# One program without barriers between its four stages, with the first query heads moved forward, two rotation buffers and a later turn of the routings

## The reference

```python
x = x + tanh(g_xattn[0]) * L0_xattn(_layernorm(x), ctx, ctx, ...)   # linear attention, 8 heads of 64
x = x + tanh(g_ffn[0])   * L0_ffn(_layernorm(x), ...)               # base product plus low-rank experts
x = x + tanh(g_xattn[1]) * L1_xattn(_layernorm(x), ctx, ctx, mask)  # 32 query heads, 8 key/value heads
x = x + tanh(g_ffn[1])   * L1_ffn(_layernorm(x), ...)               # sign(weight) product, routed scales

# L1_xattn, the stage in which the kernel spends half of its time
q = apply_rope((query @ Wq).reshape(b, t, 32, 128))
k = apply_rope((key @ Wk).reshape(b, t, 8, 128))
v = (value @ Wv).reshape(b, t, 8, 128)
logits = einsum('btkgd,bTkd->bkgtT', q, k) * 0.0884
logits = where(mask, 30 * tanh(logits / 30), -1e30)
out = einsum('bkgtT,bTkd->btkgd', softmax(logits), v).reshape(b, t, 4096) @ Wo

# L1_ffn
routing = softmax(xf @ gate_w.T)
out = (xf * (routing @ in_channel_scale)) @ sign(weight).T * (routing @ out_channel_scale) + bias
```

## Time and profile before

| | |
|---|---|
| median of 3 runs | 3259.19 us (3249.48 to 3260.86) |
| profiled execution | 3252.94 us, span 3250.9 us, granted clock 0.972 |
| busy, TensorE | 3068.2 us, 94% of the span |
| busy, VectorE | 2013.4 us, 62% |
| busy, GpSimd | 1924.7 us, 59% |
| busy, ScalarE | 1228.9 us, 38% |

### The profile page before, as it was taken

How to read it: one execution, slowest core, us unless ns; L and a number is a source line. 1 busy time by engine, 2 the same in 40 slices (tenths; PEclk the granted TensorE clock), 3 DMA queues, 4 the chain that set the end, 5 groups by cost and what they waited for, 6 DMA issues and landing times. The chain is left out here.

```text
span 3250.9 us, 41151 instructions
## 1 busy us (share of the span) xinstructions
PE 3068.2 (94%) x14547; PEld 2465.2 (76%) x14547; DVE 2013.4 (62%) x2509; ACT 1228.9 (38%) x1898; POOL 1924.7 (59%) x1342
## 2 busy tenths in 40 slices
PE   7999779999999996799999999999999999999799
PEld 6888558787887875687877787777878787877577
DVE  3332257777777763576666666676767676666575
ACT  3111145555555552343333433333333333343232
POOL 4222354555555543677777777777777777774343
PEclk9999889999999997899999999999999999998899
DMA  7343511112121124222244232343222432223221
GB/s 201 103 135 108 179 35 40 53 66 79 39 79 53 66 76 146 91 104 92 102 149 149 97 115 94 112 170 122 103 90 103 152 146 97 104 94 134 91 72 52
DMA packets 187912, 332.49 MB, mean 102 GB/s; under 512 B 10585, under 2 KB 103129, under 8 KB 185737
## 3 DMA queue, kind: packets, MB, share of 16 engines
q1 hardware_dynamic: 187784, 330.82, 29.7%
HBM read 255.29 MB, written 75.50 MB: 102 GB/s over the span
## 5 line engine op out<-in xcount | busy, mean ns | idle before, releaser
L1834 DVE RECIPROCAL g_rsum<-pair 128x512 f32<-128x512 f32 x128 | 429.7, 3357 | 114.3 <-PE pair L1908 111.0
L1873 PE MATMUL pair<-g_xn_hi,g_wq_hi 128*128 128x512 f32 x1024 | 400.0, 391 | 10.3 <-issue 10.3
L1873 PE MATMUL pair<-g_xn_lo,g_wq_hi 128*128 128x512 f32 x1024 | 399.7, 390 | 0.0
L1873 PE MATMUL pair<-g_xn_hi,g_wq_lo 128*128 128x512 f32 x1024 | 399.5, 390 | 0.0
L1932 PE MATMUL pair<-g_wo_hi,g_at_hi 128*128 128x512 f32 x992 | 386.0, 389 | 0.0
L1932 PE MATMUL pair<-g_wo_lo,g_at_hi 128*128 128x512 f32 x992 | 385.9, 389 | 0.0
L1932 PE MATMUL pair<-g_wo_hi,g_at_lo 128*128 128x512 f32 x992 | 385.8, 389 | 0.0
L1820 DVE SCALAR_TENSOR_TENSOR g_res<-pair,g_tg,g_res 128x512 f32<-128x512 f32 x256 | 189.8, 747 | 205.0 <-PE pair L1932 203.3
L1575 POOL TENSOR_TENSOR g_wq_lo<-g_wq_raw,g_wq_hi 128x1024 fp32r<-128x1024 f32 x129 | 307.1, 2405 | 4.3 <-ACT g_wq_hi L1713 4.2
L1713 ACT ACTIVATE g_q_hi<-g_q_raw 128x512 fp32r<-128x512 f32 x128 | 81.0, 633 | 542.7 <-POOL g_q_raw L1652 542.7
L1652 POOL TENSOR_TENSOR g_q_raw<-g_q_raw,g_rot_b 128x512 f32<-128x512 f32 x128 | 227.4, 1776 | 97.7 <-DVE g_rot_b L1805 97.7
(11 more groups left out here) (250 smaller groups left out, 7261.6 us busy)
## 6 DMA issues: line engine op xcount, KB each, us to landing
g_wq_raw<-in_L_Wq SPq DMA_DIRECT2D x64, 1024.0 KB, 7.2
g_wo_raw<-in_L_Wo SPq DMA_DIRECT2D x62, 1024.0 KB, 6.5
values_split<-c_v SPq DMA_DIRECT2D x64, 256.0 KB, 2.8
keys_split<-c_k SPq DMA_DIRECT2D x32, 512.0 KB, 2.7
xn_turned<-a_x2T SPq DMA_DIRECT2D x16, 1024.0 KB, 7.7
g_k<-keys_split SPq DMA_DIRECT2D x32, 512.0 KB, 3.3
g_v<-values_split SPq DMA_DIRECT2D x32, 512.0 KB, 7.3
c_cx_raw<-in_ctxT SPq DMA_DIRECT2D x16, 512.0 KB, 7.4
```

The lines of the kernel that those rows point to most:

```text
L1834: V.reciprocal(rsum[:, :], p_sum[:, :]).then_inc(rsum_done, 1)
L1873: mm = M(bank[:, :], w[a][:, i, cols], x[b][:, i, :], start=(i == 0 and t == 0), stop=(i == KT - 1 and t == 2))
```

## The change

1. The four blocks become one. Each stage now returns a function for each engine, and every engine runs the four one after another, with no barrier. In place of the barriers stand counters: `front_over` and `layer_over` (4 engines report; GpSimd then clears the old semaphores and makes the next stage) and `cleared`, for which the others wait before they use the new stage. GpSimd's clearing moves from the start of a stage into it.
2. Query head 0 of the attention (24 matmuls) is projected inside step 16 of layer 0, query head 1 in two halves of 12 matmuls in step 17. For this the weights' low halves are made by GpSimd (two quarters) and VectorE (two quarters) in step 16, and SP issues the loads of `xn` before, not after, step 16's stores. At the attention's start only heads 2 and 3 are left.
3. There are two rotation buffers; heads 0 and 2 use one, 1 and 3 the other, and `rotate` waits for the addition of head i−2 only.
4. In the feed-forward stage the turns of the routings stand behind the last two `out_scale` of a pair, not before them.

```diff
@@ linear_attention_moe_stage, SP
             for s in range(0, BATCH + 3 + 1):
                 if s == BATCH:
+                    sp.wait_ge(cleared, 1)
                     sp.wait_ge(gathered, KT * BATCH)
                     g.early["sync"][0]()
-                step(s)
-                if s == BATCH:
                     sp.wait_ge(qproj, KT * BATCH)
                     sp.wait_ge(turned["q"], KT * BATCH)
                     sp.wait_ge(out_done, 2 * BATCH)
                     sp.wait_ge(n_store, 16 * 4)
                     g.early["sync"][1]()
+                step(s)
@@ linear_attention_moe_stage, GpSimd
             def step(s):
+                nonlocal g
+                if s == 2:
+                    pool.wait_ge(front_over, 4)
+                    nc.clear_and_free_semaphores(spent)
+                    g = next_stage()
+                    pool.sem_inc(cleared, 1)
@@ linear_attention_moe_stage, TensorE
+            front_drained(pe, 1)
             pe.wait_ge(vo_in, 32)
...
             mm.then_inc(avo_made, 1)
+            front_drained(pe, 3)
+            pe.sem_inc(front_over, 1)
...
+                if s == BATCH + 1:
+                    g.early["pe"][1]()
                 h_turn(s - 2)
...
                 gather(s, 6)
+                if s == BATCH:
+                    pe.wait_ge(cleared, 1)
+                    g.early["pe"][0]()
                 x_turn(s - 1, 0)
...
+                if s == BATCH + 1:
+                    g.early["pe"][2]()
                 n_turn(s - 2, 0)
@@ gqa_stage
-    rot_b, rsum = sb("rot_b", [P, BANK]), sb("rsum", [P, BANK])
+    rot = [sb("rot_b", [P, BANK]), Arena(nc, "g_", FLOOR + 204 * 1024)("rot_b1", [P, BANK])]
+    rsum = sb("rsum", [P, BANK])
...
-        nc.gpsimd.tensor_tensor(dst, dst, rot_b[:, :], ALU.add).then_inc(rot_done, 1)
+        nc.gpsimd.tensor_tensor(dst, dst, rot[i % 2][:, :], ALU.add).then_inc(rot_done, 1)
...
-        dve.wait_ge(rot_done, FIRST + n * NR + i)
+        if i >= 2:
+            dve.wait_ge(rot_done, FIRST + n * NR + i - 1)
...
+    def first_head():
+        for done in (q_proj, s_done, sum_done, pv_done, y_done):
+            pe.sem_inc(done, 1)
+        for i in range(HALVES):
+            pe.wait_ge(land["xn"][i], 64)
+        pe.wait_ge(wq_lo, FIRST + 4)
+        projection(p_proj[0], wq, slice(0, HD), xn).then_inc(q_proj, 1)
+
+    def second_head():
+        projection(p_proj[1], wq, slice(HD, 2 * HD), xn, rows=range(KT // 2))
+
+    def second_head_rest():
+        projection(p_proj[1], wq, slice(HD, 2 * HD), xn, rows=range(KT // 2, KT)).then_inc(q_proj, 1)
...
-            project(0, 0)
+            project(0, heads_=range(2, G))
@@ sign_ffn_stage, TensorE
                 main(p, 3, 1)
+                for u in range(2, 4):
+                    if q:
+                        out_scale(p + 1, u)
                 if r:
                     turn_routing(2 * p + 4)
                     turn_routing(2 * p + 5)
-                for u in range(2, 4):
-                    if q:
-                        out_scale(p + 1, u)
```

More of the change, by code:

```diff
@@ L1810, in first_dve @@
             dve.sem_inc(done, 1)
+        for m in range(2, 4):
+            dve.wait_ge(wq_hi, FIRST + m + 1)
+            subtract_hi(V, wq, part("wq", m // 2, m % 2)).then_inc(wq_lo, 1)
     def add_output(n_out, u):
@@ L1865, in gqa_stage, with projection @@
     M, T = nc.tensor.matmul, nc.tensor.transpose
-    def projection(bank, w, cols, x, fresh=None):
-        for i in range(KT):
+    def projection(bank, w, cols, x, fresh=None, rows=range(KT)):
+        for i in rows:
             if fresh is not None and i % 2 == 0:
@@ L2609, in flamingo_layers, with make_second, make_third, _ @@
                                        xnT)
-    run_kv(first.early)
-    second = first.run(kv_sems, lambda: gqa_stage(nc, banks, kept_tiles, x2, xnT, k_split, v_split, a["gate_x1"],
-                                                  a["L1_Wq"], a["L1_Wo"], x3))
-    third = second.run(first.sems, lambda: sign_ffn_stage(nc, banks, x3, a["gate_f1"], a["L1_signT"], a["L1_bias"],
-                                                          a["L1_gateT"], a["L1_in_scale3"], a["L1_out_scale3"], out))
-    third.run()
+    later = {}
+    def make_second():
+        later["second"] = gqa_stage(nc, banks, kept_tiles, x2, xnT, k_split, v_split, a["gate_x1"], a["L1_Wq"],
+                                    a["L1_Wo"], x3)
+        return later["second"]
+    def make_third():
+        later["third"] = sign_ffn_stage(nc, banks, x3, a["gate_f1"], a["L1_signT"], a["L1_bias"], a["L1_gateT"],
+                                        a["L1_in_scale3"], a["L1_out_scale3"], out)
+        return later["third"]
+    keys_values, layer0 = run_kv(first.early), first.run(kv_sems, make_second, front_drained)
+    block = stack.enter_context(nc.Block())
+    @block.gpsimd
+    def _(_):
+        keys_values["gpsimd"]()
+        layer0["gpsimd"]()
+        later["attention"] = later["second"].run(first.sems, make_third)
+        later["attention"]["gpsimd"]()
+        later["ffn"] = later["third"].run(later["second"].sems)
+        later["ffn"]["gpsimd"]()
+    @block.sync
+    def _(_):
+        for stage in (keys_values, layer0, later["attention"], later["ffn"]):
+            stage["sync"]()
+    @block.scalar
+    def _(_):
+        for stage in (keys_values, layer0, later["attention"], later["ffn"]):
+            stage["scalar"]()
+    @block.vector
+    def _(_):
+        for stage in (keys_values, layer0, later["attention"], later["ffn"]):
+            stage["vector"]()
+    @block.tensor
+    def _(_):
+        for stage in (keys_values, layer0, later["attention"], later["ffn"]):
+            stage["tensor"]()
     stack.close()
```

139 lines of the change are left out of this document (61 added, 78 removed).

## The result

The changed kernel took 3226.65 us (median of 4 runs, 3220.78 to 3229.41) beside 3257.84 for the kernel before (4 runs, 3249.48 to 3260.86): a ratio of 0.9909, 95% interval 0.9893 to 0.9924, or 30 us. The forecast was 3236. The profiled execution took 3229.41 us with a span of 3227.6, so its distance from the one before (3250.9) is only 23.3.

A forecast was written before the change was run, and what follows sets the result against it. TensorE, at 94% of the span, bounds the kernel, with 63 us of touchable waits. Terms −0.4 + 2.4 − 18.6 − 0.5 − 2.8 = −19.9 give 3233 on the profiled run, 3239 on the median; forecast 3236 us, range 3214 to 3252.

The forecast's parts named there:

- The attention's steps: Attention's 31 steps: second rotation buffer ends the last low part 0.64 us earlier each; −18.6 us, bounds −4 and −23.8.
- rival C: Attention steps: GpSimd's chain of additions sets the end, 0.13 to 0.2 a step; total −5 to −9, some 3247; chance 0.18.
- The second boundary: Layer 0 to the attention: early matmuls save 7.8 us, a delayed store takes 10.2 back; +2.4, bounds −8 and +6.
- the held store: Layer 0's tail: row 12's store behind eight loads delays TensorE's turn of h(14); +15.4 until the lora product.
- gaps that the early heads fill: Layer 0's tail: heads 0 and 1 fill TensorE gaps of 4.79 and 3.63, keeping the clock up; +15.4 becomes +10.2.
- the 48 matmuls: Attention's start: query heads 0 and 1 already made in layer 0 save 7.8 us there.
- Rival B: All three boundaries pay the idle they show, less what barriers leave: about −20 more, some 3213; chance 0.12.
- The first and third boundaries: Keys/values to layer 0, and attention's end: loads hold the next work, only barrier passing goes; −0.4 and −0.5 us.
- The pair ends: Feed-forward stage: two out_scale matmuls cover 0.7 us of the routing wait at three pair ends; −2.8, bounds 0 and −8.
- a little where the clock would not fall: Feed-forward pair ends: small extra gain from the clock, taking −2.2 to −2.8.
- Rival E: Layer 0's tail: store delay not given back, plus a second for row 13; +15 to +20, some 3253; chance 0.08.

The follow-up runs named there:

- experiment 1: Kernel before with only the second rotation buffer added: 3236.41 us, ratio 0.9945 to the kernel before.
- experiment 5: Changed kernel with the store of x2T's row 12 issued ahead of the eight xn loads: 3217.6 us, ratio 0.9879 to the kernel before.
- experiment 4: Changed kernel with no query head made in layer 0, loads still ahead of row 12's store: 3226.05 us, ratio 0.9911 to the kernel before.
- 9: Changed kernel with row 12's store ahead of the loads and no query head made in layer 0: 3211.72 us, ratio 0.9876 to the kernel before.
- 12: Changed kernel with row 12's store, x's row 1 and gate load earlier, wb splits in step 1, no early heads: 3197.56 us, ratio 0.9823.
- Experiment 10: Kernel before with only the barriers gone, but the query weights' low parts made as in the changed kernel: 3242.32 us, ratio 0.9965.
- Experiment 6: Changed kernel with x's row 1 loaded first at layer 0's start, ahead of constants and wb: 3222.3 us, ratio 0.9895 to the kernel before.
- experiment 3: Kernel before with only the routing turns moved behind a pair's last two out_scale: 3242.43 us, ratio 0.9963.

## Why the prediction was right, and where it was not

**The attention's steps: right, in mechanism and size.** Forecast was a last low part 0.64 us earlier in each step; the plain steps went from 52.64 to 52.00 us. The schedule worked out holds row by row when 6.5 us are taken off: split until 2049.7 (measured 2043.14), addition of head 2 until 2050.8 (2044.31), last low part until 2056.12 (2049.60). Which of VectorE and GpSimd goes next when both wait was read from two rows, and it decided between −0.64 and −0.13; rival C is out. Forecast −18.6, measured by itself −18 (experiment 1). In the profiled pair it was only −14.6, since the step behind the second group change waited 3.27 us for the probabilities' low part and met a lower clock. The two periods there take 106.4 us before, 109.9 after, and 105.3 to 109.0 in the other kernels with two buffers, so this isn't a stable part of the change; why it varies stays open.

**The second boundary: right in its sum, wrong in its parts.** Forecast +2.4, measured +1.8, and on the way the keep of row 13 at 1241.7 (1239.90), the tanh at 1298.2 (1297.77), the first rotation at 1298.5 (1298.01), head 2's start at 1300.6 (1300.16). The price of the held store is shown by experiment 5 (9 us). But the forecast had it at 15.4, brought down to 10.2 by gaps that the early heads fill and by the clock that this keeps up, and then took 7.8 back for the 48 matmuls; experiments 4, 9 and 12 show that the heads are worth nothing once the barrier is gone. Without them (experiment 4) the last residual comes 8.5 us later than before, with them 10.5: no gap was filled to a profit, and the gap of 3.63 before the turn of h(15) isn't there in either. Two things were left out. One is the move of the low parts, which frees VectorE's routing and takes 4 to 5.5 us off. The other is the barrier: it kept TensorE standing 10.28 us beside work for which all was ready. The forecast had asked of each barrier what is late behind it for the whole chain, and for this one had not asked what TensorE could do in the meantime. Experiment 10 gives −11, both together, for what the forecast summed to a few tenths. That the sum came out right is in good part luck: one term credited to the heads stood for these two. Rival B was right about this one boundary and wrong about the other two.

**The first and third boundaries: right.** VectorE's statistics of row 1 started at 408.72 (before 409.51), the wait for the query maxima was 22.3 us as forecast ("over 20"), and the wait at the third is 9.6 in place of 10.0. Experiment 6 shows the named load as the cause: moved ahead, it lets VectorE start at 390.96.

**The pair ends: mis-sized.** The term was −2.8, with −8 as its bound; by itself it measured −12 (experiment 3), −9.5 in the traces. The waits shrank by 0.6 us each (1.23 to 0.65), and a pair without a fall of the clock by the 0.7 that was forecast (25.4 to 24.65), at five ends and not three. What the step called "a little where the clock would not fall" is the greater part of the rest: a pair with a fall took 1.5 to 3 us more. The trace of before showed the falls; I priced them as chance, and they go with the long waits, eight of twelve.

Together: the parts measured alone give −11 (barriers and the low parts' move), −18 (buffer) and −12 (pair ends), −41. The held store takes back 9, and 32 are left, of which 30 were measured; the early heads add nothing. Each of these is known to some 4 us. The forecast came out 9 us too high, and the pair ends' term alone was 7 to 9 too small. Rival E's price was about half of what it said, and it was outweighed.

## What to carry to other kernels

A wait shown behind a barrier has two prices, what the chain behind it gains, and what the waiting engine could do in the meantime: ask for the second too before moving work ahead by hand, since the free engine may do it unasked. When a list of DMAs moves ahead of a store in one queue, follow the store's landing to the buffer that it frees. And where TensorE's waits of about a microsecond stand in front of a lower granted clock, price the slow stretch behind the wait with it: here the waits at four pair ends shrank by 2 us together and the stage by 9.5. When small VectorE instructions on the chain take 2 us each, look at what GpSimd does beside them before you touch anything else.

## What the runs showed that I had not expected

With waits of 0.63 to 0.95 us at the pair ends TensorE's granted clock never fell behind one (51 of them in eleven traces); with waits of 1.23 it fell behind eight of twelve, and the stage took 7 to 11 us less in every trace with the new order than in those with the old. Idle of 13.67 us before the third query head brought the clock to its lower level for the next nine or so (0.63 us each for 0.39), while with 48 matmuls made in that gap (experiment 4) the slow ones were among those, and the third head's first took 0.50; so work made early can cost as much as it saves. In each of the three pairs of traces with and without early heads the tail is 4 to 6 us longer with them, though by the ratios the kernels differ by less than 4 us, within the uncertainty. The eight loads of the attention's input took 12.0 us to issue (13.2 before), and a store behind them was held for all of it.
